# Feed-forward stage: blocks of 32 pixels turned by VectorE, and second-layer products set between the next chunk's first-layer products

## The reference

```python
xi = _omni(xf..., ffn_alpha, ffn_w1, ffn_w3, ffn_w5)
xf2 = xi.reshape(B, C, T).transpose(0, 2, 1)
kk = jnp.square(jax.nn.relu(xf2 @ ffn_wk.T))      # 192 -> 768
kv = kk @ ffn_wv.T                                # 768 -> 192
ffn_out = jax.nn.sigmoid(xf2 @ ffn_wr.T) * kv     # gate: 192 -> 192
tok = tok + gamma2 * ffn_out                      # back to NCHW
```

## Time and profile before

| | us |
|---|---|
| median of 3 runs | 5778.59 |
| span of the profiled execution | 5771.5 |
| feed-forward stage, its first gate matmul | starts at 3990.12 |
| last residual addition of the stage | starts at 5767.87 |

### The profile page before, as it was taken

How to read it: one execution, slowest core, us unless ns; L and a number is a source line. 1 busy time by engine, 2 the same in 40 slices (tenths; PEclk the granted TensorE clock), 3 DMA queues, 4 the chain that set the end, 5 groups by cost and what they waited for, 6 DMA issues and landing times. The chain is left out here.

```text
span 5771.5 us, 78482 instructions
## 1 busy us (share of the span) xinstructions
PE 4950.2 (86%) x23504; PEld 3918.4 (68%) x23504; DVE 3670.1 (64%) x5128; ACT 3642.4 (63%) x7348; POOL 3545.3 (61%) x2992
## 2 busy tenths in 40 slices
PE   5979999979976776867867764997999999999999
PEld 5969999967733443443444434776888888888888
DVE  4423333367759999999999994775555555555555
ACT  0017777746657877877878774665566656555555
POOL 0017777757769888889888883775444444444444
PEclk9989999989988888988988887998999999999999
DMA  6987777679930321313223116997223223223220
GB/s 166 265 211 194 189 195 187 172 193 264 254 93 12 93 57 45 82 44 77 68 57 79 45 34 156 254 268 179 57 57 90 56 56 90 56 56 75 71 56 24
DMA packets 388599, 674.51 MB, mean 117 GB/s; under 512 B 21117, under 2 KB 346702, under 8 KB 368910
## 3 DMA queue, kind: packets, MB, share of 16 engines
q1 hardware_dynamic: 334768, 514.71, 38.3%
q10 hardware_dynamic: 53522, 156.21, 7.2%
HBM read 437.00 MB, written 233.87 MB: 116 GB/s over the span
## 5 line engine op out<-in xcount | busy, mean ns | idle before, releaser
L1580 POOL TENSOR_TENSOR hidden_part<-hidden_whole,hidden_part 128x448 fp32r<-128x448 f32 x672 | 751.8, 1153 | 1024.2 <-ACT hidden_part L1545 1024.2
L676 POOL TENSOR_TENSOR omni_in_part<-omni_norm,omni_in_part 113x448 fp32r<-113x448 f32 x384 | 601.2, 1577 | 210.1 <-ACT omni_in_part L735 207.5
L1449 PE MATMUL f_out_ps<-hidden_part,ffn_wv_parts 128*128 128x448 f32 (+1 forms) x3360 | 720.2, 370 | 0.7 <-POOL hidden_part L1580 0.7
L1449 PEld LDWEIGHTS f_out_ps<-hidden_part,ffn_wv_parts 128*128 128x128 f32 (+1 forms) x3360 | 578.1, 177 | 103.1 <-POOL hidden_part L1580 35.2
L1623 DVE TENSOR_SCALAR hidden_whole<-f_hid_ps 128x448 f32<-128x448 f32 x672 | 417.5, 622 | 252.1 <-POOL hidden_part L1580 153.0
L87 PE MATMUL omni_ps<-omni_in_part,omni_band_part 113*112 113x448 f32 x1152 | 439.7, 382 | 111.1 <-POOL omni_in_part L676 78.4
L1050 PE MATMUL proj_ps<-mixT_low,kvr_weights_low 128*128 128x448 f32 x672 | 354.6, 612 | 205.5 <-ACT k_all L1114 161.3
L1235 POOL TENSOR_TENSOR input_times_v<-input_factor,v_all 128x448 f32<-128x448 f32 x336 | 420.1, 1250 | 159.4 <-ACT input_factor L1119 144.9
L1052 PE MATMUL proj_ps<-mixT_ends,kvr_weights_ends 128*128 128x448 f32 x1008 | 512.0, 591 | 0.0
L87 PE MATMUL dw_ps<-dw_in_part,dw_band_part 112*112 112x432 f32 (+3 forms) x1344 | 474.5, 353 | 42.1 <-POOL dw_in_part L477 42.1
L88 PE MATMUL dw_ps<-dw_in_part,dw_band_part 112*112 112x432 f32 (+3 forms) x1344 | 474.8, 353 | 0.0
(11 more groups left out here) (181 smaller groups left out, 13290.0 us busy)
## 6 DMA issues: line engine op xcount, KB each, us to landing
xin<-x SPq DMA_DIRECT2D x16, 2352.0 KB, 13.2
x_pointwise<-xp ACTq DMA_DIRECT2D x16, 2352.0 KB, 18.9
dw_in<-x_pointwise SPq DMA_DIRECT2D x24, 1568.0 KB, 24.4
y_gelu<-dw_out ACTq DMA_DIRECT2D x24, 1568.0 KB, 13.2
omni_in<-y_gelu SPq DMA_DIRECT2D x24, 1568.0 KB, 22.9
att_mix<-omni_out ACTq DMA_DIRECT2D x24, 1568.0 KB, 13.3
residual_pairs<-y_gelu SPq DMA_DIRECT2D x16, 2352.0 KB, 11.8
tok<-residual_pairs SPq DMA_DIRECT2D x16, 2352.0 KB, 9.0
```

The costliest lines, as they stand in the source:

```text
L676: pool.tensor_tensor(rounded(inner(p[1])), z[u][:, :, cc, :], inner(p[0]), ALU.subtract).then_inc(in_split, 1)
L1449: return pe.matmul(bank, rounded(w), rounded(x), start=start, stop=stop)
L1580: pool.tensor_tensor(rounded(kk[n % 2][1][:, h, :]), whole[h % KW][:, :], kk[n % 2][0][:, h, :], ALU.subtract).then_inc(kl_ready, 1)
```

## The change

It touches `feed_forward` only, and there four things.

1. *Loads.* The 112 pixels are cut into slots of 32 (the fourth holds 16 pixels twice, the second copy shifted by one row pair). A slot is loaded by quadrants: 32 channels x 32 pixels on each group of 32 partitions. That is 12 transfers of 32x4x224 for slots 0 to 2 and 24 smaller ones for slot 3, 60 an image in place of 2. There is one buffer for each slot, not two; a slot is loaded again when its last chunk has been turned.
2. *Turning.* VectorE's transpose of 32x32 blocks, three a chunk over 128x448 (`mix` low, both ends together, `tok` low), from SBUF to SBUF with a source step of 28 elements. A chunk is now 32 pixels wide and 14 row pairs long. TensorE's 16 turns and their four banks go. The low rest of `mix` moves from VectorE to GpSimd.
3. *Order.* In step s TensorE takes the gate of chunk s+1, then hidden block h of chunk s+1 and the five second-layer products h of chunk s in turn. There are three hidden banks, one bank for the gate, and two pairs for the output; the gate's end products of chunk n use the pair of chunk n-2.
4. *Finish and stores.* VectorE finishes chunk s at the end of step s, with the first 128 channels first and then the end. The residual now comes from SBUF, so both inputs of line 1731 are in SBUF. Results gather in half images, stored in 2 transfers per half.

```diff
+            def receptance(i, n):
+                pe.wait_ge(x0_split, at(i, 1, n + 1 + 2))
+                pe.wait_ge(x1_split, at(i, 1, n + 1))
+                pe.wait_ge(g_ready, at(i, 2, 2 * n + 1))
+                of_input(n, r_ps[0:C0, 0:TC], ...).then_inc(r_ready, 1)
-                    pe.wait_ge(gv_done, i * (CH * 2) + (2 * n - 1 + 4))
-                    bank = v_ps[1][:, 0:TC]
+                pe.wait_ge(gv_done, at(i, 2, 2 * n + 2))
+                bank = v_ps[n % 2][1][:, 0:TC]
                 (3 products of the gate's end into bank)
+            def hidden(i, n, h):
+                pe.wait_ge(relu_done, at(i, HT, HT * n + h - HB + 1 + HT))
+                of_input(n, h_ps[h % HB][:, 0:TC], ...).then_inc(h_ready, 1)
+            def outputs(i, n, h):
+                if h == 0:
+                    pe.wait_ge(g_ready, at(i, 2, 2 * n + 2 + 2))
+                    pe.wait_ge(gv_done, at(i, 2, 2 * n + 1))
+                pe.wait_ge(kl_ready, at(i, HT, HT * n + h + 1 + KW))
...
+            def body(i, s):                      # TensorE
+                more = exists(i, s + 1)
+                if more:
+                    receptance(i, s + 1)
+                for h in range(HT):
+                    if more:
+                        hidden(i, s + 1, h)
+                    if s >= 0:
+                        outputs(i, s, h)
...
+            def body(i, s):                      # ScalarE
+                if exists(i, s + 1):
+                    gates(i, s + 1)
                     for h in range(HT):
+                        square(i, s + 1, h)
+                        if h in (1, 2):
+                            high_of_mix(i, s + 2, h == 2)
+                if s >= 0:
+                    rest_of_out(i, s)
...
+            def finish(i, n):                    # VectorE
+                for c in range(2):
+                    if c == 0:
+                        dve.wait_ge(v_ready, at(i, 2, 2 * n + 2 + 4))
+                        dve.wait_ge(g_ready, at(i, 2, 2 * n + 2 + 2))
+                    else:
+                        dve.wait_ge(v_rest_ready, at(i, 1, n + 1))
+                        dve.tensor_add(banks[1], banks[1], v_rest[:, :]).then_inc(v_summed, 1)
+                        dve.wait_ge(v_summed, at(i, 1, n + 1 + 1))
+                    dve.wait_ge(res_done, at(i, 2, 2 * n + c + 1))
+                    dve.tensor_mul(gv[c][rows, :], banks[c], sg[n % 2][c][:, :]).then_inc(gv_done, 1)
...
+            def body(i, s):                      # VectorE
+                if exists(i, s + 1):
+                    sum_r(i, s + 1)
+                    clip(i, s + 1, 0)
+                    turn_mix(i, s + 2)
+                    clip(i, s + 1, 1)
+                    turn_ends(i, s + 2)
+                    clip(i, s + 1, 2)
+                    rest_of_end(i, s + 2)
+                    clip(i, s + 1, 3)
+                    turn_tok(i, s)
+                    for h in (4, 5):
+                        clip(i, s + 1, h)
+                else:
+                    turn_tok(i, s)
+                if s >= 0:
+                    finish(i, s)
```

More of the change, by code:

```diff
@@ L1421, in feed_forward, with at, image_of, steps @@
         res_done = m.sem("result_ready")
-        stored = [m.sem(f"result_stored{u}") for u in range(2)]
+        stored = [m.sem(f"result_stored{n}") for n in range(2)]
         block = ctx.enter_context(nc.Block())
         CH = 2 * NCH
+        PAIRS = B // 2
         W_LOADS = 128
[L1427 to L1432, removed]
+        def at(i, per, count):
+            return i * (CH * per) + count
+        def image_of(i, n):
+            return i * 2 + n // NCH
+        def steps(eng, body):
+            body(0, -1)
+            with eng.Fori(0, PAIRS - 1) as i:
+                for s in range(CH):
+                    body(i, s)
+            for s in range(CH):
+                body(PAIRS - 1, s)
+        def exists(i, n):
+            return not isinstance(i, int) or CH * i + n < CH * PAIRS
+        def pixels(n):
+            slot, half = ORDER[n % NCH]
+            return ([[2, PJ // 2], [PJ, BLK]], slot * SLOT) if slot == 3 else (
+                [[1, PJ // 2], [PJ, BLK]], slot * SLOT + half * (PJ // 2))
         @block.tensor
@@ L1436, in _ @@
             pe.wait_ge(w_split, 8)
[L1438 to L1446, removed]
             def product(bank, w, x, start, stop=False):
@@ L1512, in _ @@
+            def body(i, s):
[7 more added lines that the diff above has]
+                        outputs(i, s, h)
+            steps(pe, body)
         @block.scalar
@@ L1647, in _, with quadrant @@
+            turn_mix(0, 0)
+            turn_ends(0, 0)
+            rest_of_end(0, 0)
+            steps(dve, body)
         @block.sync
         def _(sp):
+            row = B * G * PJ
+            QG = BLK // G
+            def quadrant(t, q, slot, src, first, image, signal):
+                reversed_rows = src is mix_d
+                p0 = (80 - BLK * slot if slot < 3 else 0) if reversed_rows else BLK * slot
+                base = first * PXC * row + p0 * row
+                to = t[q * BLK:(q + 1) * BLK, slot * SLOT:(slot + 1) * SLOT].rearrange("p (g r) -> p g r", g=QG)
+                pieces = [(0, BLK, 0)] if slot < 3 else [(0, 16, 0), (16, 32, 1)]
+                for lo, hi, skip in pieces:
+                    run = G * PJ - skip
+                    sp.dma_start(to[lo:hi, :, 0:run],
+                                 dram(src, sp.snap(image * (G * PJ) + (base + skip)) if not isinstance(image, int)
+                                      else image * (G * PJ) + base + skip,
+                                      [[row, hi - lo], [PXC * row, QG], [1, run]])).then_inc(signal, 16)
@@ new lines, in store @@
+            def store(i, n):
+                half = 0 if n % NCH == 3 else 1
+                sp.wait_ge(res_done, at(i, 2, 2 * n + 2 + 2))
+                for c in range(2):
+                    where = [i * (2 * C * HW) + ((n // NCH) * C * HW + c * C0 * HW + half * HALF)]
+                    if not isinstance(i, int):
+                        where = [sp.snap(a) for a in where]
+                    sp.dma_start(dram(out, where[0], [[HW, (C0, C1)[c]], [1, HALF]]),
+                                 res[c][rows_of[c], half * HALF:(half + 1) * HALF]).then_inc(stored[half], 16)
@@ L1649, in _ @@
+            load_mix(0, 0)
             for n, rows in ((0, (0, C0)), (1, (0, C1)), (1, (C1, 128))):
```

348 lines of the change are left out of this document (188 added, 160 removed).

## The result

The changed kernel takes 5915.74 us (median of 4 runs, 5908.68 to 5918.32); the kernel before, run beside it, 5780.89 (5777.19 to 5785.06). The ratio is 1.0234, 95% interval 1.0222 to 1.0247. The forecast was 5795, in a range of 5750 to 5875: slower as forecast, but by 135 us where I had 16, and outside the range. The profiled execution spans 5914.1 us against 5771.5, so 142.6 us have to be found.

The account below looks back on a forecast made before the run. TensorE was taken as the bound. Turns, waits, pause and ends: -221 - 9 + 234 + 9 = +13 on 5771.5, so 5784.5; 7.1 more for the median and 3 for small terms gave 5795 us, range 5750 to 5875.

Parts of the forecast that it names:

- What goes, -221 - 9: On TensorE, turns and small waits go, 1.97 us in each of 112 chunks (221 us), and 9 at the loop's turns.
- What comes, the pause: TensorE waits once a chunk before the gate's end products for VectorE's finishing chain: 2.13 us, 234 us in all.
- E: The time at which the gate's first product on TensorE starts or could start; the pause's steps are read from it.
- square 0.64 after the clip: On ScalarE, in the chain to the pause: the square starts 0.64 us after the last clip, which starts at E - 0.74.
- The contention rival: GpSimd's subtraction delays VectorE's residual addition of the first channels: pause about 1.3 us longer, 143 us, so 5938; chance 0.09.
- The lower bound of 1.71: The pause if ScalarE's way costs nothing and VectorE's instructions follow each other at 0.62: 1.71 us, or 188 us.
- the short pause: Rival: VectorE's chain runs without ScalarE's delay and without gaps, so the change pays: -33 us, 5745; chance 0.14.
- no wait at all: Case in which the wait before the gate's end products did not bind: 5579 us, said to be excluded by the counts.
- turns of 2.5 us: Rival: VectorE's transposes at 2.5 us each bound the stage, about 17.5 us a chunk: 5990; chance 0.05.
- The clock stays: Against the rival that TensorE's clock falls at each pause, losing 2 us a chunk: +220, so 6015; chance 0.04.
- Costs put at nothing: VectorE's three transposes a chunk (0.62 to 1.15 us each), GpSimd's added subtraction and the 60 loads an image: all hidden.
- The ends, +9: Start and end of the stage: +3 for the first gate matmul, +1 filling, +2 and +3 at the last chunk.

Follow-up runs that it names:

- the kernel with ten dummies: The changed kernel with ten extra 448-column matmuls in the pause, their results overwritten: 5820.57 us.
- VectorE's order: The changed kernel with VectorE's subtraction for the next mix end behind the fourth clip and the turn of tok behind the third: 5907.23 us.
- the two edits together: The changed kernel with ScalarE's rest-row copy ahead of its last square and VectorE's first-128-channel residual addition behind the second gate multiplication: 5697.44 us.
- the end first: The changed kernel with ScalarE's rest-row copy ahead of its last square and VectorE finishing the last 64 channels first: 5734.77 us.
- the last version: The changed kernel with own gate-end bank, VectorE's order, first sigmoid waiting for its half's reader only, weights' transfers ahead of mix's first slot: 5571.24 us.
- the bank alone: The changed kernel with a PSUM bank of their own for the gate's end products, hidden blocks keeping two banks: 5625.9 us.
- the last two versions: The changed kernel with own gate-end bank, VectorE's order and first sigmoid waiting for its half's reader only, without and with weights' transfers first: 5582.59 and 5571.24 us.
- the kernels with two dummies: The changed kernel with two extra 448-column matmuls in the pause, their results overwritten: 5816.64 us.
- TensorE's order of before: The changed kernel with all six hidden blocks of the next chunk, then all six blocks of second-layer products: 5796.0 us.

## Why the prediction was wrong

**What goes, -221 - 9: right.** At 0.2022 a matmul, 68 take 13.75, and 15.846 - 13.75 = 2.10 a chunk, 229 us for 109 chunks, went with the turns and waits. (In unbroken stretches matmuls start 0.2035 apart on average, not 0.2022; over 68 that is 0.09 us, which stands in the 0.24 below.)

**What comes, the pause: right place, right chain, too small.** One pause a chunk, released by `gated` L1724, and 0.24 beyond it. I had put that 0.24 down to starting again. Of it the trace shows 0.10 there (one matmul of the first three behind the restart starts 0.31 after the one before in place of 0.20) and 0.09 spread over the chunk, and the kernel with ten dummies keeps all of it with a pause of 0.15. So it fits as a term of the sum, but its cause is only in part shown. The sum 13.75 + pause + 0.24 gives 16.14 (measured 16.15) for the changed kernel, 15.94 (15.96) for VectorE's order, 15.12 (15.12) for the two edits together and 15.26 (15.27) for the end first. But I forecast 1.89 + 0.24 and it is 2.15 + 0.24: 0.26 x 109 = 28 us. The clip was right (E - 0.81 for my E - 0.74). The step that was mis-sized is "square 0.64 after the clip", and with it ScalarE's copy at E + 1.00: it is 0.91, because the clips before come late and close together and ScalarE is still rounding the block before. They are late because `rest_of_end` waits 1.7 us for ScalarE, and I gave that wait no row in the chain. The contention rival came half true, by the same cause: L1731 takes 1.04 in the median in place of 0.62, but ends only when ScalarE's copy does, and alone costs nothing. As I priced it, with GpSimd's last subtraction just ahead, it stands in seven chunks of the kernel with VectorE's order: a pause of 3.04 for 1.95, so 1.1 where I had 1.3.

Three numbers of the forecast don't follow from its own working. The lower bound of 1.71 leaves out the 0.24 that the 2.13 contains; like for like it is 1.95, and the short pause would have stood at about 5771 and not 5745. With no wait at all the sum is 5795 - 234 = 5561, not 5579. And turns of 2.5 us give (17.5 - 15.9) x 110 = 176 on top, about 5970, not 5990.

**"The clock stays": the step that failed.** I priced this rival nearly right (2 us for a fall, measured 1.57) and gave it 0.04. The argument against it, "nearly 14 us of unbroken matmuls lie between two pauses", was no evidence: it says nothing of what one pause does. I had two rows, a pause of 2.28 without the fall and one of 2.78 with it, and read 2.1 as safe; two rows say nothing of how often. What the runs showed in its place: 64 of 109 chunks lose the clock behind pauses of the same length as in the 45 others (median 2.19 in both), at 1.57 us each, and filling the pause gives that 100 us back. With 0.59 of the chunks at 1.57 and a pause of 2.39, the sum is -229 + 261 + 100 + 9 = +141, against 142.6.

TensorE: Matmul & The Clock Gate in the Trainium skill ("A second HAM failure mode: psum-queue depth-cycling") tells of a kernel whose engine idles briefly between groups of matmuls, so that the clock goes back and forth. The trace agrees, 64 of 109 chunks. It would have been a reason for a much higher chance.

**Costs put at nothing: right for what was listed.** A transpose of VectorE takes 1.06 us, between my 0.62 and 1.15, and in the last version TensorE waits for clips in only 12 places of 1200 us. Not listed were the 1.73 that VectorE stands in front of the subtraction L1681, and its 1.38 in place of some 0.62. The groups by line of the changed kernel, 4200 to 5700 (busy us, mean ns, idle before):

```profile
L1667 DVE STREAM_TRANSPOSE ffn_mixT_low<-ffn_mix_low 128x448 f32<-128x448 f32 x88 | 93.1, 1058 | 0.0
...
L1681 DVE TENSOR_TENSOR ffn_mix_end<-ffn_mixT_tokT_ends,ffn_mix_end 64x448 fp32r<-64x448 f32 x88 | 121.1, 1376 | 151.9 <-ACT ffn_mix_end L1562 151.9
L1731 DVE TENSOR_TENSOR result<-gated,ffn_tokT_low 128x448 f32<-128x448 f32 x88 | 87.0, 988 | 4.0 <-DVE gated L1724 1.1
```

**The ends, +9: +9.4 measured**, by luck: the start was +6.7 for my +3, filling -8.3 for my +1, the end +11.0 for my +5.

## What to carry to other kernels

When a change trades spread work of TensorE for one repeated pause, price the clock as a term of the sum and not as a remote rival; a test with a few dummy matmuls in the pause tells its share in one run. When two paths meet at a wait, edit both before judging either. And look for the bank that makes the wait: here one of eight, moved, was worth 290 us and turned a loss of 2.3% into a gain of 2.7%.

## What the hardware showed that I had not expected

- Pauses of 1.95 to 2.15 us once a chunk: clock lost in 64 to 69 of 109 chunks (four kernels). Pauses of 1.71 and 1.77: in 4 and 3. Of 1.27: in 5. Of 1.13 or 0.15: in none. No regular pause: in 2 with the bank alone, in none of the last two versions.
- Those 14 falls all stand behind a single longer stop, of 1.97 us or more, all at a turn of the loop. Of 172 pauses of 1.65 to 1.85 in the kernels with two dummies and with TensorE's order of before, none was followed by a fall; of 96 pauses of 1.85 to 2.03 in the kernel with VectorE's order, 61 were. It isn't a clean edge: 9 of the 264 falls of the four kernels stand behind a shorter pause, 0.88 to 1.78.
- The length of the pause does not tell which chunk falls. In the changed kernel they come in a nearly fixed pattern, three in five (chunks 4, 6, 7, 9, 11, 12, 14, 16, 17, 19 and so on, counted from 0). What makes the pattern these runs don't show.
- In the steady chunks each fall lasts 3.41 us, whatever the pause, and 36 of the 64 start within 0.4 us of the restart in the changed kernel.
- A VectorE operation with two SBUF inputs that starts while GpSimd is in a subtraction ends about 0.48 us after GpSimd's does. L1681 takes 1.40 us in the median where GpSimd has 0.93 left, and 0.78 where it has 0.30 left (the kernel with the bank alone and TensorE's order of before); L1731 takes 1.04 with 0.56 left and 1.53 with 1.05 left. Where VectorE starts first, L1731 takes 0.63 and GpSimd's subtraction 1.38 in place of 1.16. Operations with one SBUF input stay at 0.62.
- At a turn of the loop the engines stand for up to 2.7 us (VectorE) and TensorE for 2.2, in the kernel with the bank alone; in the changed kernel the pause had hidden that from TensorE.
